# A mixture-of-experts layer on one core: the lead expert is found after the first quarter, its weights are loaded in eight separate pieces, and two row loads move behind the inputs

## The reference

```python
def _L0_cond_ref(x, w, b):        # x (8, 512, 1024), w (8 taps, 1, 1024)
    y = jax.lax.conv_general_dilated(x, w, window_strides=(1,), padding=[(K - 1, 0)],
            feature_group_count=D, dimension_numbers=('NWC', 'WIO', 'NWC'))
    return y + b
def _L0_ffn_ref(x, w_router, w_experts):      # E = 8 experts, H = 1024
    logits = jnp.einsum('bsh,eh->bse', x, w_router)
    idx = jnp.argmax(logits, axis=-1)
    all_out = jnp.einsum('bsh,efh->bsef', x, w_experts)
    return jnp.take_along_axis(all_out, idx[:, :, None, None], axis=2)[:, :, 0, :]
x = x + _L0_ffn_ref(_L0_cond_ref(x, cond_2048[:, None, :], L0_cond_b), ...)
```

## Time and profile before

| what | us |
|---|---|
| median of 3 executions | 549.53 (548.73 to 549.76) |
| the profiled execution's own time | 547.22 |
| its span | 545.4 |
| PE busy in the span | 509.8 (93%) |
| PE in convolution products | 123.8 |
| PE in expert products | 385.7 |

### The profile page before, as it was taken

One profiled execution on the slowest core, in us unless ns is written; L12 is line 12 of the kernel. 1 busy time (PEld: TensorE's weight loads), 2 busy tenths in 40 slices (PEclk: granted clock), 3 DMA queues, 4 the chain that ended last, 5 costly groups with the idle time before them and its releaser, 6 DMA issues.

```text
span 545.4 us, 9396 instructions
## 1 busy us (share of the span) xinstructions
PE 509.8 (93%) x2740; PEld 441.0 (81%) x2741; DVE 285.7 (52%) x376; ACT 151.4 (28%) x255; POOL 135.6 (25%) x148
## 2 busy tenths in 40 slices
PE   5999999876899945999999999999999999999995
PEld 5999999876688834888888888888888888888884
DVE  4945473464895105229976432295229422492761
ACT  2343434534200001006653100061006100160620
POOL 0004132070261102122233131222222222122312
PEclk9999999977899995999999999999999999999999
DMA  8977979996298995546999955479647964436344
GB/s 284 412 183 243 359 226 389 282 325 262 77 373 238 403 329 147 177 119 230 353 378 367 284 176 170 121 241 330 194 119 241 332 192 121 149 117 191 115 145 163
DMA packets 59477, 130.30 MB, mean 239 GB/s; under 512 B 12736, under 2 KB 32576, under 8 KB 59456
## 3 DMA queue, kind: packets, MB, share of 16 engines
q1 hardware_dynamic: 41840, 70.32, 41.6%
q0 software_dynamic: 14832, 54.27, 27.7%
q10 hardware_dynamic: 2784, 5.46, 3.4%
HBM read 94.56 MB, written 35.45 MB: 238 GB/s over the span
## 4 chain that ended last, share of the span: by engine, by line
PE 77%; DMA 11%; SPq 5%; issue 3%; DVE 2%; POOL 2%; ACT 0%; POOLq 0%; DVEq 0%
PE ps L817 61%; PE ps L775 15%; DMA xs<-x_t 6%; DMA ids_all<-y_sorted 3%; SPq L282 2%; DMA xs<-x_both 2%; SPq L382 2%; POOL y_sorted L873 1%; DMA y_sorted<-rows,pos_i 1%; DVE x_row L668 0%; SPq L304 0%; SPq L313 0%; DVE xs L498 0%; SPq L284 0%; SPq L294 0%
## 5 line engine op out<-in xcount | busy, mean ns | idle before, releaser
L817 PE MATMUL ps<-w_sb,ys 128*128 128x512 f32 x1680 | 385.7, 392 | 15.2 <-DVE ys L660 12.7
L817 PEld LDWEIGHTS ps<-w_sb,ys 128*128 128x128 f32 x1680 | 318.1, 190 | 82.2 <-issue 15.8
L775 PE MATMUL ps<-mats,xs 128*128 128x128 f32 x1024 | 123.8, 285 | 14.4 <-DVE xs L498 8.6
L655 DVE STREAM_TRANSPOSE y_cols<-y_blk 128x1024 f32<-128x1024 f32 x36 | 44.8, 1243 | 175.5 <-PE ps L817 144.7
L775 PEld LDWEIGHTS ps<-mats,xs 128*128 128x128 f32 x1024 | 122.0, 201 | 15.2 <-DVE xs L498 9.2
L434 ACT CAST ys<-y_cols 128x1024 fp32r<-128x1024 f32 x36 | 37.9, 1052 | 287.5 <-DVE y_cols L655 275.3
L885 POOL DMA_INDIRECT out<-x_row,idx x35 | 43.5, 1243 | 109.2 <-DVE x_row L668 106.4
L646 DVE TENSOR_TENSOR w_sb<-w_raw,w_sb 128x1024 fp32r<-128x1024 f32 x56 | 64.3, 1221 | 3.2 <-ACT w_sb L429 3.2
L429 ACT CAST w_sb<-w_raw 128x1024 fp32r<-128x1024 f32 x56 | 56.4, 1052 | 9.5 <-PE ps L817 8.4
L892 POOL COPY idx<-ids_all 128x1 int32 (+1 forms) x36 | 15.7, 436 | 172.6 <-DMA out<-x_row,idx 98.6
L873 POOL DMA_INDIRECT y_sorted<-rows,pos_i x32 | 36.3, 1134 | 82.6 <-PE ps L775 56.3
(11 more groups left out here) (95 smaller groups left out, 35.6 us busy)
## 6 DMA issues: line engine op xcount, KB each, us to landing
w_raw<-experts SPq DMA_DIRECT2D x56, 512.0 KB, 8.8
y_blk<-y_sorted SPq DMA_DIRECT2D x152, 128.0 KB, 2.6
xs<-x_both SPq DMA_DIRECT2D x15, 512.0 KB, 9.7
xs<-x_t SPq DMA_DIRECT2D x28, 256.0 KB, 6.3
xs<-x_t ACTq DMA_DIRECT2D x20, 256.0 KB, 6.2
w_first<-experts SPq DMA_DIRECT2D x8, 512.0 KB, 14.5
ids_all<-y_sorted SPq DMA_DIRECT2D x38, 1.0 KB, 3.5
x_row<-x_rows,idx POOLq DMA_INDIRECT x36, 4.5
```

What stands on the lines that cost most here:

```text
L655: V.transpose(y_cols[k][:, :, :].rearrange("p m (t i) -> p t m i", t=4), y_blk[:, k, :, :, :]).then_inc(y_blocks, 1)
L775: mm = nc.tensor.matmul(to, xs[:, n % X_RING, s % PACK, :], mats[:, s, :].rearrange("p (u n) -> p u n", n=SIDE), start=(s == sets[0]), sto ...
L817: mm = nc.tensor.matmul(out_ps[k][:, f * HALF:(f + 1) * HALF], ys[k][:, a, c, :], w_sb[:, c, b, f * HALF:(f + 1) * HALF], start=(c == 0 an ...
```

## The change

Five things change.

- `find_lead` runs in the second quarter (`g == 1`), from the first quarter's counts. A new `second_slot` runs in the third, `third_slot` stays in the last; both use a common `next_slot`. All stand directly behind `place_rows`, and `place_rows` itself now stands after the fourth `double` of the quarter, where it stood after the seventh.
- The eight `w_first` chunks are issued behind the loads of packs 30, 34, ... 58, one each (`W_AT`).
- The rows of slots 0 and 1 are loaded when SP has issued its last x.
- Slot 5's rows are loaded between `w_raw[0]` and `w_raw[1]`.
- The factors of packs 2 to 15 come in three transfers instead of two, the last one (packs 8 to 15) behind x of packs 4 and 5.

```diff
-FACTOR_PACKS = [(0, 1), (1, 2), (2, 8), (8, PACKS)]
+FACTOR_PACKS = [(0, 1), (1, 2), (2, 4), (4, 8), (8, PACKS)]
-Y_AFTER = [(LAST + 1) * PACKS - 4, (LAST + 1) * PACKS - 2]
+W_AT = range(PACKS + X_RING + 6, GROUPS * PACKS, 4)
...
+            load_x(sp, 4)
+            load_x(sp, 5)
+            load_factors(4)
+            for n in range(6, GROUPS * PACKS):
+                if n == W_AT[0]:
+
+                    sp.wait_ge(lead_known, 1)
+                    e = sp.value_load(one_i[0:1, 0:1], min_val=0, max_val=EXPERTS - 1)
+
+                    sp.wait_ge(mats_ready, PACKS + 1)
                 if not on_second_queue(n):
                     load_x(sp, n)
...
+                if n in W_AT[:HC]:
+                    c = W_AT.index(n)
+                    sp.dma_start(w_first[:, c, :], chunk(e, c)).then_inc(first_in[c], 16)
+
+            for t in range(FIRST):
+
+                sp.wait_ge(lead_known, t + 1)
+                row = lead_row(t)
+
+                sp.wait_ge(y_out[t % 2], (t // 2 + 1) * TPG * 16)
+                if t < RING:
+
                     sp.wait_ge(w_split, t + 1)
-                    load_y(sp, lead_row(t), t, ids_all[:, t:t + 1, :])
...
+                else:
+                    sp.wait_ge(y_blocks, t - 1)
+                load_y(sp, row, t % RING, ids_all[:, t:t + 1, :])
...
-            sp.wait_ge(y_blocks, FIRST + 1)
-            load_slot(FIRST + 2, (FIRST + 2) % RING)
+                if k == 0:
+
+                    sp.wait_ge(y_blocks, FIRST + 1)
+                    load_slot(FIRST + 2, (FIRST + 2) % RING)
...
+            def next_slot(most):
+
+                step(V.tensor_tensor(count, base, const(C_BASE), ALU.subtract))
+                step(V.scalar_tensor_tensor(out=done, in0=count, scalar=most, in1=lead, op0=ALU.min, op1=ALU.mult))
+                step(V.tensor_reduce(limit, done, AX.X, ALU.add))
+                step(V.tensor_scalar(one[:, 7:8], limit, full_row, -float(P), ALU.add, ALU.add))
+                return one[:, 7:8]
+
+            def second_slot():
+
+                row = next_slot(float(2 * P))
+                step(V.tensor_scalar(limit, limit, float(P), None, ALU.add))
+                V.tensor_copy(lead_i[:, 1:2], row).then_inc(lead_known, 1)
...
-                for k in range(3, 7):
-                    double(n + k)
+                double(n + 3)
                 place_rows(g - 1)
-                double(n + 7)
...
+                if g == 1:
+                    find_lead()
+                elif g == 2:
+                    second_slot()
                 else:
                     third_slot()
```

More of the change, by code:

```diff
@@ L72 @@
 LAST = GROUPS - 1
-FIRST = (LAST - 1) * GT // EXPERTS // P + 1
-MOST_SLOTS = (TOKENS + EXPERTS * (P - 1)) // P
+FIRST = 3
+MOST_SLOTS = FIRST + (TOKENS - P + EXPERTS * (P - 1)) // P
 RING = 2
-Y_AFTER = [(LAST + 1) * PACKS - 4, (LAST + 1) * PACKS - 2]
-ROUNDS = -(-(MOST_SLOTS + 1 - FIRST) // RING)
+W_AT = range(PACKS + X_RING + 6, GROUPS * PACKS, 4)
+ROUNDS = -(-(MOST_SLOTS - FIRST) // RING)
 SLOTS = FIRST + ROUNDS * RING + 3
@@ L255, in build @@
         route_step = sem("route_step")
-        first_known = sem("first_known")
-        third_known = sem("third_known")
+        lead_known = sem("lead_known")
         rows_ready = sem("rows_ready")
@@ L338, in _ @@
             load_factors(3)
-            early = (LAST - 1) * PACKS + X_RING + 10
-            for n in range(4, early):
+            load_x(sp, 4)
[6 more added lines that the diff above has]
+                    sp.wait_ge(mats_ready, PACKS + 1)
                 if not on_second_queue(n):
                     load_x(sp, n)
[L344 to L359, removed]
-                    sp.wait_ge(w_split, t + 1)
-                    load_y(sp, lead_row(t), t, ids_all[:, t:t + 1, :])
[L363 to L368, removed]
+                if n in W_AT[:HC]:
[6 more added lines that the diff above has]
+                if t < RING:
+                    sp.wait_ge(w_split, t + 1)
+                else:
+                    sp.wait_ge(y_blocks, t - 1)
+                load_y(sp, row, t % RING, ids_all[:, t:t + 1, :])
             sp.wait_ge(rows_ready, 1)
@@ L564, in find_lead @@
                 step(V.tensor_reduce(full_row, tmp, AX.X, ALU.add))
-                V.tensor_scalar(lead_i[:, 0:2], const(C_SPLIT, 2), full_row, None, ALU.add).then_inc(first_known, 1)
-            def third_slot():
[L569 to L573, removed]
+                V.tensor_copy(lead_i[:, 0:1], full_row).then_inc(lead_known, 1)
+            limit = one[:, 6:7]
+            def next_slot(most):
[8 more added lines that the diff above has]
+                V.tensor_copy(lead_i[:, 1:2], row).then_inc(lead_known, 1)
+            def third_slot():
+                V.tensor_copy(lead_i[:, 2:3], next_slot(limit)).then_inc(lead_known, 1)
             def count_slots():
@@ L693, in _ @@
                 choose(g - 1)
-                for k in range(3, 7):
-                    double(n + k)
+                double(n + 3)
                 place_rows(g - 1)
-                double(n + 7)
[L698 to L702, removed]
+                if g == 1:
+                    find_lead()
+                elif g == 2:
+                    second_slot()
                 else:
                     third_slot()
[L705 to L708, removed]
+                for k in range(4, 8):
+                    double(n + k)
+                for k in range(8, PACKS, 2):
+                    if g == LAST:
+                        low(0, k // 2 - 4, w_first)
+                    double(n + k)
+                    double(n + k + 1)
                 if g < LAST:
```

## The result

The changed kernel takes **534.85 us** (four executions, 533.70 to 536.23) against 549.51 us (the kernel before, now with four executions). The ratio is 0.9736, 95% interval 0.9711 to 0.9762, so 14.7 us less. I had forecast 528.5 us, range 521.5 to 539.0. The direction and the range held.

A forecast was written before the change was run, and what follows sets the result against it. Bound by PE's idle stretches and lower clock: late x (14.7 us) and slot 5's rows (12.70 us gap). Terms -7.2 before the first product and -13.8 after give -21.0, from 549.53 to 528.5 us, range 521.5 to 539.0.

The forecast's parts named there:

- late x in the convolution's last quarter: Convolution from 100.34 us on: 14.7 us lost to gaps and slower pace, all of which the change recovers, -14.7 us.
- From the start to the first product: Everything before the first product: six terms, -14.7 - 1.2 + 5.0 + 1.7 + 1.0 + 1.0, sum to -7.2 us.
- From the first product to the end: Product stage: -15.5 at slot 5 and +1.7 at slot 6 sum to -13.8 us.
- The start: First packs: x of pack 4 lands earlier with 512 KB of factors moved behind it, -1.2 us, between 0 and -1.5.
- Three new waits: After each `rank`, PE's fifth pack waits for a DVE copy behind `place_rows` and the search, +5.0 us in sum.
- The clock: Convolution: the new 2.5 us gap lowers PE's granted clock and slows the packs after it, +1.7 us, ends 0 and 3.
- x among chunks and scatter: Convolution: x loads are delayed by weight chunks and the last quarter's unbraked scatter, +1.0 us, ends 0 and 5.
- the prediction's sentence for the other view: Convolution queues: a chunk holds back only what follows on its own queue, so x's term is nearer 0, time 527.5 us.
- Slots 0 and 1: Before the first product: rows issued at pack 54 need 12.7 us with 11.7 left, +1.0 us, ends 0 and 5.
- Slot 5 and 6: Product stage: slot 5's gap and lower clock go, -15.5 us; slot 6 is late next, +1.7, ends 0 and 5.
- a sign of being wrong: Product stage: the prediction counts as wrong if slot 6 waits over 5 us.
- The wait only moves to slot 6: Rival, product stage: slot 6's rows come 6 us late and the clock falls, 8.8 instead of 1.7, 535.6 us; chance 0.12.

The follow-up runs named there:

- e5: The changed kernel with DVE's copies for each quarter's fifth to seventh pack put back ahead of `place_rows` and the lead search; 529.34 us, ratio to before 0.9669.
- e3: The changed kernel with the third expert's eight weight chunks issued behind slot 6's rows; 529.29 us, ratio to before 0.9665.
- e4: The changed kernel with slot 0's rows issued behind x of pack 60 and slot 1's behind pack 62, as before the change; 536.59 us, ratio 0.9781.
- r1: The changed kernel itself, unaltered, timed again in a second series beside the kernel before; 533.90 us, ratio 0.9755.
- e1: The changed kernel with slot 5's rows put back behind all 16 chunks of the next two experts; 540.61 us, ratio to before 0.9853.
- e7: The changed kernel with the third quarter's eight scatters each held until one further pack of PE is done; 534.14 us, ratio to before 0.9766.
- e11: The changed kernel with the factors in four transfers as before, the last ahead of x of pack 4; 535.78 us, ratio to before 0.9778.
- e10: The kernel before with one part of the change alone, the rows of slots 0 and 1 loaded behind all x; 544.93 us, ratio 0.9966.

## Why the prediction was right and where it was off

**Right in kind.** What bounded the kernel was read correctly: late x in the convolution's last quarter and slot 5's rows behind 8 MB of weights. Both waits went. From the start to the first product the forecast was 7.2 us less, and the two profiled executions have 4.5 and 6.6. From the first product to the end it was 13.8 less, and both have 6.5 (397.9 and 397.8 us against 404.4). So most of what is missing is missing in the product stage.

**The start**, forecast -1.2: -0.3 to -0.65. The size was off: the packs after the fifth gave part of the gain back, as x of pack 6 landed at 18.21 and PE's pack 6 started right then.

**Three new waits**, forecast 2.5, 1.3 and 1.1 to 1.2, sum 5.0: measured 2.02, 1.16 and 1.04, sum 4.2, and the same within 0.02 us in every profiled execution with this order of copies. The working was right and 0.8 us too long; 0.3 of it is `find_lead`, which took 2.07 us here (43.12 to 45.19) where it had taken 2.4. That it is a plain loss, which e5 shows, was what the sum said.

**The clock**, forecast +1.7 with ends 0 and 3: it is there in the first profiled execution, 28.69 - 27.07 = 1.6 us, and in those of e3 and e4. It is not in r1, e1, e7 and e11, which do the same work up to there and ran the 15 packs in 27.07. So it is chance here, and the forecast's value and its lower end both occur. No run tells what decides it.

**x among chunks and scatter**, forecast +1.0: the last 12 packs should take 21.7 us, and took 22.7 (108.09 to 130.75) in one and 21.70 in r1. No x was late, although DVE waited for it; the 1.0 us of the first is not x but pauses called issue (see Open). So this term is 0, as the prediction's sentence for the other view had it (nearer 0). That the sum up to the convolution's end came out near is partly luck: in the first execution pauses that nobody had in mind fill this term, and in r1 it and the clock's are both missing. The convolution ended at 130.75 (128.56 in r1), where the forecast's terms give 138.44 - 14.7 - 1.2 + 5.0 + 1.7 + 1.0 = 130.2.

**Slots 0 and 1: the first step that failed.** The forecast put +1.0 here. The gap is 5.75 (5.88 in r1) instead of 2.55, so the term is 3.2 to 3.3. The need was right: 7.0 us from landing to first product means 4.4 us before the end of the convolution. What was mis-sized is the time that was left. I had the rows issued 16 us before the convolution's end; they were issued 14.2 us before it in r1 (114.37 to 128.56) and 12.5 in the first execution (118.25 to 130.75). The landing, 12.7 us from an issue at pack 54, was about right (114.37 to 127.44 is 13.1; 118.25 to 129.51 is 11.3). e10 shows what this step overlooked: rows could be slow at no cost as long as x was late, and when x was in time they took back 5.7 of 7.6 us. I had sized this as a remainder.

**Slot 5 and 6: the second step.** The -15.5 came, as the gap at slot 5 went, and slots 0 to 5 run at their pace but for a small new gap of 1.15 us ahead of slot 3 (0.66 ahead of slot 4 in r1). What is late next was named rightly, slot 6. Its size was wrong: forecast 1.7 with the slower pace, ends 0 and 5; measured 5.72 and 1.7 (209 products in 49.32 us, where 0.228 each makes 47.6), 7.4 together. That is also what I had named as a sign of being wrong, a wait of over 5 us at slot 6, and it is the rival "The wait only moves to slot 6" (8.8 us, 535.6), which had got a chance of 0.12: its 8.8 us and its 535.6 are nearer to what was measured than the forecast's 1.7 and 528.5. The forecast holds by its range, not by this step. I had let the queue be empty at the same moment as before, with the same bytes in it. But slot 7's rows and the transfers of a slot that PE now works are in it too, 1.0 MB more, and from the first chunk to the landing it is 39.9 us instead of 34.6 (38.4 in r1). e3 shows that the 4 MB ahead of slot 6's rows are the condition: behind them the gap is there, ahead of them it is not. That slot 7's rows lengthen it is argued from the bytes; no run takes them out alone.

The two steps make up 2.2 + 5.7 us, the small gap 1.15 and the convolution's end 0.5. That is 9.6 of the 10.0 us by which the profiled span lies above the forecast 524.4. The median lies 6.3 above. The profiled execution was the longest of its four.

**Open.** PE's trace shows single products with pauses of 0.2 to 1.1 us called issue between 112 and 119 us in the changed kernel's first profiled execution and in e1 to e4, all four runs of the first series. The 12 packs behind the third `rank` take 1 us longer than 21.7 in the first, 3.9 in e1, 2.5 in e3 and 5.2 in e4. DVE has pauses of the same name at that time, as `114.06 0.68 DVE L496` with 1.92 us in the changed kernel's. r1, e5 to e11 and the kernel before have none. So they seem to go with the series and not with an edit, and no run tells what they are. They blur every comparison with the first series, above all e4's.

## What to carry to other kernels

When a transfer is moved ahead of others in a full queue, write down for the next one in it what will be in the queue by then, with the engines running on and not standing. The wait that was taken away had also kept other transfers back (slot 7's rows). When a search or table step is moved up, check what the producer of the next tile still owes: here three copies in each quarter that cost nothing ahead of a wait cost 4.6 us behind it. And weights that are needed late can stand behind rows that are needed soon: the third expert's were issued from 175.85 on and first read at 250.79.

## What the runs showed of the hardware that I had not expected

The same gap of 2.02 us, after the same work, left TensorE at 2.4 GHz in four profiled executions (r1, e1, e7, e11) and was followed by slower packs, at a cost of 1.6 us, in three (the changed kernel's first, e3, e4).

A full queue is not one rate. The DMA share is 1.02 at 412 GB/s with weights in it, and 1.13 at 214 GB/s five microseconds later with the rows of two slots.
